# Expert and permuted layers of a four-layer program: the first thread's steps up to its gates are put into the units of the attention ahead, the second thread 38 units of the table behind it

## The reference, cut to what matters

```python
x = x + L0_xattn(_layernorm(x), ctx_4096, ctx_4096)      # a: correlation attention
x = x + L0_ffn(_layernorm(x), weight, bias)              # a: quantized product
x = x + L1_xattn(_layernorm(x), ctx_4096, ...)           # b: attention, 32 query heads, 8 key heads
x = x + L1_ffn(_layernorm(x), W_base, b_base, W_gate, W_thr, b_thr, A_w, B_w)   # c: experts
x = x + L2_xattn(_layernorm(x), ctx_4096, ctx_4096, Wt, Wp, Wg, Wz, gn_w, gn_b) # c: grouped products
x = x + L2_ffn(_layernorm(x), up, down, perm)            # c: permuted ffn
x = x + L3_xattn(_layernorm(x), ctx_4096, ...)           # d: attention with rope
x = x + L3_ffn(_layernorm(x), w1, w2, w3)                # e: swiglu, 4-bit weights
# L1_ffn (experts):
gate = softmax(xf @ W_gate.T); thr = sigmoid(xf @ W_thr + b_thr[0]) * 0.125
w = (gate - thr) * (gate >= thr); w = w / sum(w)
out = x @ W_base.T + b_base + einsum('ner,ne,eor->no', einsum('nd,erd->ner', xf, A_w), w, B_w) * 2.0
# L2_xattn: t = Wt v, p = Wp q, g = Wg k by channel; att = sum(p * g) in each of 8 groups;
#   y = Wz (att * t); group norm of y, * gn_w + gn_b, + v      (q = norm of x, k = v = ctx)
# L2_ffn: t = x[:, perm]; per head (16): gelu(t @ up) @ down; then unpermuted
```

## Time and profile before

| what | us |
|---|---|
| median of 3 runs | 2120.04 |
| lowest and highest run | 2106.90, 2120.16 |
| the profiled execution, its own time | 2114.82 |
| its span in the profile | 2112.7 |

### The profile page before, as it was taken

One profiled execution on the slowest core, in us unless ns is written; L12 is line 12 of the kernel. 1 busy time (PEld: TensorE's weight loads), 2 busy tenths in 40 slices (PEclk: granted clock), 3 DMA queues, 4 the chain that ended last, 5 costly groups with the idle time before them and its releaser, 6 DMA issues.

```text
span 2112.7 us, 26355 instructions
## 1 busy us (share of the span) xinstructions
PE 1807.0 (86%) x8645; PEld 1468.2 (69%) x8645; DVE 1504.1 (71%) x2735; ACT 1072.4 (51%) x2556; POOL 1038.2 (49%) x889
## 2 busy tenths in 40 slices
PE   5664799999999999774967689999999999878879
PEld 3443677788788788662744568888888888656757
DVE  6667489989989985547343578888888888747740
ACT  2433477777777775422334245555555543335630
POOL 3665265655655654413132257776776742016720
PEclk7997899999999999966866799999999999989989
DMA  3002111111121120020002011111111110111120
GB/s 114 6 1 77 45 41 50 61 51 46 55 61 46 46 65 16 23 84 1 0 1 75 25 31 51 36 36 51 36 42 45 36 50 1 42 30 50 38 69 35
DMA packets 53991, 88.00 MB, mean 42 GB/s; under 512 B 8992, under 2 KB 15648, under 8 KB 53600
## 3 DMA queue, kind: packets, MB, share of 16 engines
q1 hardware_dynamic: 53856, 86.33, 13.6%
HBM read 75.56 MB, written 10.75 MB: 41 GB/s over the span
## 4 chain that ended last, share of the span: by engine, by line
PE 30%; DVE 21%; issue 16%; POOLq 11%; POOL 8%; ACT 6%; DVEq 5%; DMA 1%; SPq 0%; ACTq 0%
POOLq L326 7%; PE c_ps L66 7%; DVE b_st_u L253 6%; POOLq L324 4%; PE a_ps L66 3%; PE d_ps_job L66 3%; PE e_ps L66 3%; PE b_ps_o L66 3%; DVEq L254 3%; PE b_ps_job L66 3%; POOL d_roped L1018 2%; PE d_ps_o L66 2%; ACT b_st_sign L234 1%; POOL c_cs L1532 1%; PE d_ps_s L66 1%
## 5 line engine op out<-in xcount | busy, mean ns | idle before, releaser
L66 PE MATMUL b_ps_o<-b_wo,b_oT 128*128 128x512 f32 x768 | 191.4, 397 | 18.5 <-DVE b_oT L1260 18.5
L66 PE MATMUL d_ps_o<-d_wo,d_oT 128*128 128x512 f32 x768 | 192.0, 399 | 9.9 <-DVE d_oT L1259 9.8
L66 PE MATMUL b_ps_job<-xnT,b_wq 128*128 128x512 f32 x768 | 192.0, 403 | 3.8 <-DVE b_qT L1260 3.2
L1018 POOL TENSOR_TENSOR d_roped<-d_rot_a,d_rot_b 128x512 f32<-128x512 f32 x80 | 104.7, 1308 | 184.2 <-DVE d_rot_b L1269 184.2
L66 PE MATMUL d_ps_job<-xnT,d_wq 128*128 128x512 f32 x768 | 192.6, 403 | 0.1
L323 POOL TENSOR_SCALAR b_pt_sign<-b_pt_sign 128x512 f32<-128x512 f32 x112 | 79.8, 712 | 210.7 <-ACT b_pt_sign L315 200.4
L253 DVE SCALAR_TENSOR_TENSOR b_st_u<-b_st_sign,b_st_u 128x512 f32<-128x512 bf16 x182 | 176.5, 970 | 9.1 <-issue 0.4
L66 PEld LDWEIGHTS b_ps_o<-b_wo,b_oT 128*128 128x128 f32 x768 | 142.5, 187 | 57.3 <-DVE b_oT L1260 24.3
L66 PEld LDWEIGHTS d_ps_o<-d_wo,d_oT 128*128 128x128 f32 x768 | 144.3, 190 | 47.9 <-DVE d_oT L1259 15.2
L66 PEld LDWEIGHTS b_ps_job<-xnT,b_wq 128*128 128x128 f32 x768 | 144.4, 193 | 35.0 <-issue 5.5
L66 PEld LDWEIGHTS d_ps_job<-xnT,d_wq 128*128 128x128 f32 x768 | 143.1, 191 | 31.1 <-PE c_ps L66 0.5
(11 more groups left out here) (366 smaller groups left out, 4505.2 us busy)
## 6 DMA issues: line engine op xcount, KB each, us to landing
b_raw<-in_wq_dram SPq DMA_DIRECT2D x32, 256.0 KB, 2.6
b_raw<-in_wo_dram SPq DMA_DIRECT2D x32, 256.0 KB, 2.8
d_raw<-in_wq_dram SPq DMA_DIRECT2D x32, 256.0 KB, 2.6
d_raw<-in_wo_dram SPq DMA_DIRECT2D x32, 256.0 KB, 2.7
e_nat<-dequantized SPq DMA_DIRECT2D x30, 256.0 KB, 3.0
b_st_v<-in_quantized_dram SPq DMA_DIRECT2D x13, 256.0 KB, 3.0
dequantized<-b_st_u SPq DMA_DIRECT2D x13, 256.0 KB, 2.8
a_ctx_in<-in_ctx_dram SPq DMA_DIRECT2D x8, 256.0 KB, 5.2
```

Of the source, the lines that this page charges most:

```text
L66: i = pe.matmul(out, a, b, start=first and t == 0, stop=last and t == len(terms) - 1)
L1018: pool.tensor_tensor(roped[:, n % 2], rot_a[:], rot_b[:], ALU.add).then_inc(s_sum, 1)
```

## The change

In `grouped_attention`: the last four units get places 7 apart instead of 10 and what drains behind them 4 apart (order only). `EARLY` becomes an argument of the same values. The splits of the first key head's four `wo` blocks, one in each of units -4 to -1 before, now all stand in unit -1 (`next_outputs`). The small tiles `ident`, `bq`, `bk`, `bv` of `b` lie behind `wo` in SBUF. `over` gets a level n, so that `c`'s steps wait only for what their tiles' memory and their x need.

In `c`: new places in `START` and `PREPARED`, and `C_AT` 49.5 lower. The first thread's context, `g`/`y`, normalisation rates and `t1` stand among `b`'s last units; `wB`, `wb`, `up`, `down` are split behind `b`'s end; `LATER` is 38. `g` and `y` use one bank each instead of two. Each thread has small tiles of its own. `E_AT` falls by 22 against `D_AT`. The two hunks that only indent `grouped_attention`'s steps are left out.

```diff
-    LATER = 52.0
-    START = {"cs": (0, 0.5), "g": (3, 1.5), "t1": (9, 1.0), "low": (13, 1.4), "gates": (19, 0), "hT": (26, 0), "ffn": (27, 3.6),
-             "norm2": (42, 0), "xs": (47, 1.3), "p": (51, 0.9), "grp": (55, 0), "y2": (58, 0.8), "x2": (58.2, 0.8), "norm3": (62, 0),
-             "t3": (67, 1.0), "pick": (71, 2.0), "up": (80, 1.5), "down": (90.5, 6.0), "out": (112, 2.0), "norm4": (121, 0), "t4": (126, 1.0)}
-    PREPARED = {"wg": -2, "wm": -1, "wp": 0, "wl": 6, "wB": 6.5, "up": 7, "tables": 7.5, "wb": 14, "down": 24}
+    LATER = 38.0
+    START = {"cs": (-14, 0.5), "g": (-11, 1.5), "rates": (-6, 0), "t1": (5, 2.2), "low": (13.5, 1.4), "gates": (20, 0), "hT": (27, 0),
+             "ffn": (33, 3.6), "norm2": (48, 0), "xs": (53, 1.3), "p": (57, 0.9), "grp": (61, 0), "y2": (64, 0.8), "x2": (64.2, 0.8),
+             "norm3": (68, 0), "t3": (73, 1.0), "pick": (77, 2.0), "up": (86, 1.5), "down": (96.5, 6.0), "out": (118, 2.0),
+             "norm4": (127, 0), "t4": (132, 1.0)}
+    PREPARED = {"wg": -13, "wm": -12.5, "wp": -12, "thr": -7, "wl": -4, "wB": 15.0, "wb": 16.0, "up": 17.0, "down": 18.0, "tables": 33}
+    EARLY, RAW, OVER = -19.0, -14.5, 13.0
...
         def gpsimd(pool):
-            yield T - 12.0
-            before(pool)
+            yield T + EARLY
+            before(pool, 0)
             pool.memset(small[:, 1], 0.0).then_inc(s_zero, 1)
...
                 for j in J:
-                    yield at(t, "t1", j)
+                    yield at(t, "ffn") - 0.5
                     if j == 0:
-                        pool.wait_ge(s_const, 16 * 6)
+                        pool.wait_ge(s_const, 16 * 5)
                     waits(pool, t, ("dve", "xn1", j))
                     done(pool.tensor_tensor(x[t][j], x[t][j], bias_b[:], ALU.add), ("xb", j))
...
                     waits(pe, t, ("pool", "cs", j))
-                    if j >= 2:
-                        waits(pe, t, ("act", "g", j - 2))
-                    done(product(pe, bank(t, j % 2), [hi_lo(wg)], [hi_lo(cs[t], j)]), ("g", j))
+                    if j:
+                        waits(pe, t, ("act", "g", j - 1))
+                    done(product(pe, bank(t, 0), [hi_lo(wg)], [hi_lo(cs[t], j)]), ("g", j))
...
-                yield at(t, "cs") - 6
-                if t == 0:
-                    before(dve)
+                for j in J:
+                    yield at(t, "g", j)
+                    waits(dve, t, ("pe", "y", j))
+                    done(dve.bn_stats(ystats[t][:, j], bank(t, 1)), ("y", j))
+                yield at(t, "rates")
+                before(dve, 4 if t else 2)
                 norm[t].rates(dve, x[t])
...
-    C_AT = B_AT + 672.0
+    C_AT = B_AT + 622.5
     D_AT = C_AT + 193.0
-    E_AT = D_AT + 662.0
+    E_AT = D_AT + 640.0
```

More of the change, by code:

```diff
@@ new lines, in steps @@
+            def steps():
+                for c in range(-HALF, units + 2):
+                    i = c % HALF
+                    if biased and 0 <= c < N_BATCH:
+                        yield at(c, 0.5)
+                        if c == 0:
+                            ready(pool, 3)
+                            pool.wait_ge(s_const, 16 * n_const)
+                        pool.tensor_tensor(resid[:, c], resid[:, c], bo[:], ALU.add).then_inc(s_xb, 1)
+                    if q_jobs(c) and rope:
+                        yield at(c, 4.6)
+                        r = rots_before(c)
+                        rope_sum(r, dve_q, max(0, q_before(c) - (i < 2)))
+                        if i > 0:
+                            yield at(c, 6.2)
+                            if i == 1:
+                                rope_sum(r + 1, dve_q, q_before(c))
+                            else:
+                                rope_sum(r + 1, dve_kv, kv_before(c))
+                    if c >= 1:
+                        yield at(c, 8.2)
+                        n, u = divmod(c - 1, pt.UNITS)
+                        if n < pt.total and u < pt.UNITS - 1:
+                            pt.sums(pool, n, u)
+                    yield at(c, 9.6)
+                    g = c // 8 + 1
+                    if next_weights_at(c):
+                        low(weight(g, "q", i))
+                        if i == 3:
+                            low(weight(g, "k"))
+                            low(weight(g, "v"))
+                    for j in next_outputs(c):
+                        if c < 0 and j == 0:
+                            pool.wait_ge(s_w, weight(0, "o"))
+                        low(weight(g, "o", j))
@@ L1062, in tensor @@
+            yield from in_order(*([split_lows(pool)] if LOWS == "gpsimd" else []), steps())
         def tensor(pe):
@@ L1256, in vector @@
+            yield from in_order(split_highs(), steps())
         def vector(dve):
@@ new lines, in vector, with over @@
+            yield from in_order(*([split_lows(dve)] if LOWS == "vector" else []), steps())
+        def over(eng, n):
+            if n < 2:
+                eng.wait_ge(s_w, PER * n_groups)
+                eng.wait_ge(dve_q, n_heads * n_groups * 2)
+                eng.wait_ge(dve_kv, n_groups * 4)
+            if n == 1:
+                eng.wait_ge(pe_pv, units - HALF)
+            if n == 2:
+                eng.wait_ge(dve_x, units - HALF)
+            if n == 3:
+                eng.wait_ge(dve_n, units)
+            if n == 4:
+                eng.wait_ge(dve_x, units)
+                eng.wait_ge(pt.s_out, 16 * pt.total)
+                if signed:
+                    eng.wait_ge(st.s_out, 16 * st.total)
@@ L1414, in expert_group_and_permuted_ffn @@
         xn = [sb("xn0", [P, 2, D]), xn1]
+        with nc.sbuf_tensor("c_small", [P, 4, P], F32) as small:
+            pass
         g_sb0 = sb("g_sb0", [P, QUAD, D])
@@ L1427, in expert_group_and_permuted_ffn @@
         acts, act_f = cs, ctx_in
+        gmax, den, weights, wsum, wzero, z, row, grp, ystats, ymv, gvar, grstd, gtmp, g_a, g_b, norm, ident = zip(vectors0, vectors1)
         ps = stack.enter_context(nc.psum_tensor("c_ps", [P, 8, 512], F32))
@@ L1661, in thread @@
                     waits(act, t, ("pe", "g", j))
-                    if t == 1 and j == 0:
-                        prepared(act, "down")
-                    done(act.copy(g_sb[t][:, j], bank(t, j % 2)), ("g", j))
+                    if j == 0:
+                        prepared(act, "down" if t else "wp")
+                    done(act.copy(g_sb[t][:, j], bank(t, 0)), ("g", j))
                 yield from turned("t1")
@@ L1772, in thread @@
                     apply("xn1", j)
-                for j in J:
-                    yield at(t, "g", j)
-                    waits(dve, t, ("pe", "y", j))
-                    done(dve.bn_stats(ystats[t][:, j], bank(t, 2 + j % 2)), ("y", j))
                 yield from turned("xn1", "t1", 2)
```

491 lines of the change are left out of this document (240 added, 251 removed).

## The result

| | before | after |
|---|---|---|
| median of 20 runs, us | 2116.8 | 2104.8 |
| lowest, highest | 2106.9, 2125.5 | 2093.2, 2111.8 |
| the profiled execution's span | 2112.7 | 2102.5 |

The ratio is 0.9939, with a 95% interval of 0.9920 to 0.9957: the change makes the kernel 12 to 13 us faster, by 0.6% (9 to 17 us by the interval). It was forecast at 2092, 25 to 28 us faster, with a range of 2072 to 2122. The direction held and the size was half; by the forecast's own bound of 1% the result is "the same". The profiles say which steps are off.

The account below looks back on a forecast made before the run. It took `b` as bound by PE and `c` by its chain of waits between engines; +3 for `b`'s start, -33 for `c` and +2 for `d` made -28, so 2092 us, with 2072 to 2122 for 8 in 10.

Parts of the forecast that it names:

- the forecast's own bound of 1%: Whole kernel: a change within 1%, about what a measurement can tell from no change, meant a time above 2099.
- `b`'s start: First units of `b`: four `wo` splits in unit -1 make the fourth load wait for a slot, +3 us.
- `b`'s own units: `b`'s units between its start and its tail: the prediction has no step for them.
- `b`'s tail: `b`'s last units, with `c`'s first steps: `b` ends 28 us later with a 13.2 us stall, `low` about 0.
- Gates to group sums: `c`, first thread: gates' chain 7 to 9 us longer beside POOL, `ffn` later, group sums +4 us.
- Group sums to last `down`: `c`, first thread: `up` at 41 us, 9 us off between `up` and first `down`, together -17 us.
- The second thread alone: `c`, after the first thread's last `down`: second thread's `up` 20 us nearer, `up` to last output unchanged at 59.8.
- `d`'s start: Start of `d`: the same four splits in unit -1 and `c`'s last turned x, +2 us.
- wait moved, not removed: Rival, `c`: second thread's own chain is late, 12 to 16 of the 20 us lost, 2104 to 2108; chance 0.20.
- DVE held up by POOL everywhere: Rival: small DVE steps beside POOL each take 1.0 us more; with 37 such steps +9, so 2129; chance 0.16.
- Full clock: Rival, `c`: granted clock stays near 1.00 instead of 0.63 and 0.70, 2078 us; chance 0.12.

Follow-up runs that it names:

- x2: The changed kernel with the four `wo` splits put back to one in each of units -4 to -1, in both attentions: 2105.2 us, ratio 0.9951.
- x1: The kernel before with only the small tiles `ident`, `bq`, `bk`, `bv` moved behind `wo` in SBUF: 2109.1 us against 2114.7, ratio 0.9973.
- x4: The changed kernel with `C_AT` 36 places later, so all steps of `c` stand behind `b`'s last unit: 2092.5 us, ratio 0.9896.
- x6: The changed kernel with `p` two places later (59 instead of 57, `grp` 62 instead of 61): 2094.2 us, ratio 0.9901.
- x3: The changed kernel with `LATER` 52 again instead of 38, and `D_AT` 14 later: 2106.5 us, ratio 0.9956.
- x5: The changed kernel with two waits added on POOL, for the first thread's gates and for the second's: 2095.7 us, ratio 0.9900.

## Why the forecast was right in direction and half in size

**`b`'s start: +3 forecast, -1.4 measured.** The load's wait is there (3.03 us) and is hidden behind `q` products; x2.

**`b`'s own units: 0 forecast, -7.1 in the profile, -4.7 in x1's.** I had not priced the tiles' move. By x1's medians (5.5 us) it is near half of the measured gain.

**`b`'s tail: right.** Stall forecast 13.2, measured 4.68 + 7.83 = 12.5. `b`'s end forecast +28, measured +31.8 behind unit 60, with the wait behind the rates at 6.0 for 6.9. `low` forecast -2 to 0, measured +1.4. The conclusion, that the tail exchanges one wait for another, is what x4 shows: 4.5 us lost at `low`, 1 us lost at `d`'s first scores.

**Gates to group sums: +4 forecast, +7.3 behind `low`.** The gates' chain grew by 5.4 where I took 7 to 9, and the first thread's last `ffn` products started at 40.7 behind `low` for 30.5 (forecast +11, measured +10.3). The loss is behind it: I let the second thread's gates cost 4 to 8, and they took 9.4 with POOL's `xs` and bias additions beside them, between the first thread's second and third `p` sums on DVE.

**Group sums to last `down`: -17 forecast, -4.3 measured (106.3 to 102.0). This step failed.** Its first half held: `up` comes 42.2 behind the group sums, 41 forecast. The second did not: I took 9 off between `up` and the first `down` because no `ffn` of the second thread stands there now. It went from 13.6 to 17.3. The `ffn` products did bound that stretch before: PE has no gap in it, and the first `down` starts behind the last `ffn` product, 3.05 us after POOL's last low:

```profile
1035.88 3.80 POOL L1532 TENSOR_TENSOR c_cs<-c_ctx_in,c_cs 128x512 fp32r<-128x512 f32 x3 [2.77 <-ACT c_cs L1701]
```
```profile
1042.73 2.93 PE L66 MATMUL c_ps<-c_cs,c_down 128*128 128x512 f32 x12
```

But without them the activations' own way over ACT and POOL is left. In after three lows are through at 1040.02, and with a fourth directly behind them (1.25) the `down` could start about 8.6 us behind `up`, by this estimate: 5 of the 9. The other 8.7 us are the second thread's steps that now stand among the first's: its rates and first `xs` ahead of the fourth cast on ACT, `xs` and an addition ahead of the fourth low on POOL, `p` ahead of `down` on PE. x6 took the last of these away (14.6); the other two are read from the traces. I read which products were gone from PE's order, and not what had moved in on ACT and POOL, in a stretch where PE is the engine that waits.

**The second thread alone: -20 forecast, -16.7 measured to the last output.** From the first thread's last `down` to the second's `up` I forecast 20, measured 18.9 (1092.44 to 1111.32), from 40.0 before: right. But from that `up` to the last output it took 64.2 instead of 59.8, and the first thread's last normalisation and turned x now stand inside the second's chunks: +4.4, "unchanged" in the forecast. In x3, where they stand ahead of that `up`, it took 56.0.

**`d`'s start: +2 forecast, +1.6 measured.**

In sum, of the -33 for `c` the trace shows -13.8 (+7.3, -4.3 and -16.7): 12.7 lost between `up` and `down`, 3.3 up to the group sums and 3.3 at the end. The unforeseen 5 to 7 us of `b` made good a part. The forecast started from the 2120 of three runs; the median of twenty is 2116.8, so that its 28 us stand as 25 against it. The rival "wait moved, not removed" gave the right time, 2104 to 2108, and the wrong place: not the second thread's own chain is late, but the first thread's, held by the second's steps on ACT, POOL and PE; that the number fits is in part luck. "DVE held up by POOL everywhere" is real at both gate chains, 5.4 and 5.2 us longer, but taking it away there (x5) brought only 3.5; how much it costs elsewhere no run shows. Its count is off as well: from 2092 to 2141 are 49 steps of 1.0, not 44. "Full clock" came for `b`'s tail alone: 0.86 for 0.63 between 888 and 933 us, and 0.76 for 0.70 from there to 1000.

## What to carry to other kernels

Two threads that share engines are brought nearer at a price: read, at the place where the leading thread waits, the order of every engine on its way (here ACT, then POOL, then PE), because the follower's steps written ahead of it there hold it; 9 of 13 us went back to the leading thread. Putting a layer's first steps into the last one's tail pays only if, in the order of the engine that bounds the tail, nothing stands ahead of data that has not landed: against all of `c` behind `b`, the same steps brought `low` 4.5 us later with the full stall and 4 earlier with a smaller one, and the early loads alone gave 4 to 5. And when executions of one program differ by as much as the change, compare the traces from a common mark before believing medians, and where the orders are equal look at the granted clock before naming a cause.

## What the runs showed of the hardware

Moving 704 bytes per partition of small tiles from ahead of `wo` to behind it, and so `wo` and the tiles between, made twelve output products of TensorE 2.88 us for 2.96 and `b` some 5 us shorter. Layer `a`, the same in all kernels here, came to its last products in 224 to 228 us with a granted clock of 0.91 to 0.92, or in 232 to 238 with 0.82 to 0.86. The same 28 products in the same order took 6.2 us in one execution, at a granted clock of 1.00, and 10.2 in another, at 0.57. And in the gates a DVE operation beside POOL lost 0.7 to 1.1 us at six steps that had two inputs in SBUF or were a TENSOR_SCALAR on SBUF, and nothing if it was a reduction or a reciprocal or read PSUM.
